# Layer-3 attention without transposes of the probabilities, and layer-1 projections in three fp16 products

## The reference

```python
# layer 1
q = (x @ Wq + bq).reshape(B, S, N_HEAD, HEAD_DIM)...   # k and v likewise
# layer 3
scores = jnp.einsum('bhqd,bhkd->bhqk', Q, K) / np.sqrt(D_HEAD)
scores = jnp.where(causal, scores, -jnp.inf)
attn = jax.nn.softmax(scores, axis=-1)
ctx = jnp.einsum('bhqk,bhkd->bhqd', attn, V)
```

## Time and profile before

| | |
|---|---|
| median of 3 runs | 2673.32 us (2670.43 to 2673.91) |
| the profiled execution's own time | 2670.77 us |
| its span | 2669.4 us |
| PE busy | 2510.5 us (94%) |
| PE weight loads busy | 2015.3 us (75%) |
| DVE busy | 2165.0 us (81%) |
| ACT busy | 2015.9 us (76%) |
| POOL busy | 1385.9 us (52%) |
| instructions | 57153 |

### The profile page before, as it was taken

How to read it: one execution, slowest core, us unless ns; L and a number is a source line. 1 busy time by engine, 2 the same in 40 slices (tenths; PEclk the granted TensorE clock), 3 DMA queues, 4 the chain that set the end, 5 groups by cost and what they waited for, 6 DMA issues and landing times.

```text
span 2669.4 us, 57153 instructions
## 1 busy us (share of the span) xinstructions
PE 2510.5 (94%) x19019; PEld 2015.3 (75%) x19019; DVE 2165.0 (81%) x7479; ACT 2015.9 (76%) x4435; POOL 1385.9 (52%) x1358
## 2 busy tenths in 40 slices
PE   7988999999999999999999999999999999999987
PEld 6756777777777777777777777777777777777766
DVE  6788888888888888888888888888888888878753
ACT  1456778887787787778788777878887887877864
POOL 2355565555556555555654555565455556545321
PEclk8889999999999999999999999999999999999999
DMA  5333233232333323233332322333232333322200
GB/s 201 104 103 94 84 101 93 85 93 78 89 90 100 94 85 93 78 90 90 101 93 84 94 78 89 90 101 93 84 94 78 90 90 105 98 82 73 56 17 21
DMA packets 178100, 237.29 MB, mean 89 GB/s; under 512 B 46032, under 2 KB 123856, under 8 KB 177424
## 3 DMA queue, kind: packets, MB, share of 16 engines
q1 hardware_dynamic: 177808, 233.64, 29.3%
HBM read 174.64 MB, written 8.45 MB: 69 GB/s over the span
## 4 chain that ended last, share of the span: by engine, by line
PE 63%; DVE 23%; ACT 6%; issue 4%; DMA 2%; SPq 2%; POOL 1%; DVEq 0%; POOLq 0%; ACTq 0%
PE bank L1397 17%; PE bank L1334 11%; PE bank L1420 8%; PE bank L1379 6%; PE bank L1436 6%; DVE PB L916 5%; PE bank L1410 4%; DVE PT L923 3%; PE bank L1322 2%; ACT AA L1181 2%; PE bank L1554 2%; PE bank L1386 2%; PE bank L1347 1%; ACT L1245 1%; DVE AA L1061 1%
## 5 line engine op out<-in xcount | busy, mean ns | idle before, releaser
L1155 ACT ACTIVATE PB<-PB,mx 128x256 f32<-128x256 f32 (+1 forms) x2048 | 835.6, 474 | 42.2 <-DVE mx L916 41.2
L556 POOL TENSOR_TENSOR BT<-BT,MN 128x1024 f32<-128x1024 f32 x256 | 545.1, 2139 | 259.2 <-DMA BT<-in_bias 254.8
L1420 PE MATMUL bank<-ident,PB 128*128 128x128 f32 x3584 | 490.4, 274 | 8.4 <-DVE PT L923 4.9
L1420 PEld LDWEIGHTS bank<-ident,PB 128*128 128x128 f32 x3584 | 423.1, 141 | 72.3 <-issue 11.7
L916 DVE CUSTOM_DVE_ANT_0 PB<-bank,caus,gain 128x128 f32<-128x128 f32 (+1 forms) x1024 | 371.0, 412 | 108.8 <-PE bank L1410 102.6
L1334 PE MATMUL bank<-TN,WS_w 128*128 128x256 f16 x3072 | 381.9, 275 | 21.8 <-ACT AA L1181 15.9
L916 DVE CUSTOM_DVE_ANT_0 PB<-bank,BT 128x256 f32<-128x256 f32 x1024 | 373.0, 419 | 29.7 <-PE bank L1410 28.1
L1410 PE MATMUL bank<-Ks,Qs 96*128 96x512 f16 (+1 forms) x1024 | 319.6, 358 | 37.3 <-DVE mx L916 26.0
L1334 PEld LDWEIGHTS bank<-TN,WS_w 128*128 128x128 f16 x3072 | 287.5, 98 | 85.2 <-ACT AA L1181 29.0
L923 DVE COPY PT<-bank 128x512 f32<-128x512 f32 (+1 forms) x512 | 315.6, 616 | 9.8 <-PE bank L1420 9.5
L1160 ACT ACTIVATE PT<-bank 128x512 f32<-128x512 f32 (+1 forms) x512 | 273.7, 535 | 28.1 <-PE bank L1420 27.6
(11 more groups left out here) (249 smaller groups left out, 4564.5 us busy)
## 6 DMA issues: line engine op xcount, KB each, us to landing
BT<-in_bias SPq DMA_DIRECT2D x256, 512.0 KB, 3.9
Qs<-QT SPq DMA_DIRECT2D x768, 32.0 KB, 1.9
Ks<-KT SPq DMA_DIRECT2D x1536, 16.0 KB, 1.8
XT<-in_xT SPq DMA_DIRECT2D x32, 256.0 KB, 2.8
X<-in_x SPq DMA_DIRECT2D x32, 256.0 KB, 3.0
AB<-ada_rows SPq DMA_DIRECT2D x32, 256.0 KB, 3.3
out<-Y SPq DMA_DIRECT2D x32, 256.0 KB, 2.0
BB<-in_wf SPq DMA_DIRECT2D x11, 256.0 KB, 3.8
```

The source lines that it names most:

```text
L556: G.op.tensor_tensor(v2(BT[k % 4]), v2(BT[k % 4]), MN[:, :].unsqueeze(1).broadcast_to([128, 2, 512]), ALU.add).then_inc(g_bt, 1)
L1155: S.op.activation(o, o, ACT.Exp, scale=-1.0, bias=mx[u.layer][:, c:c + 1]).then_inc(a_exp, 1)
L1420: last = T.op.transpose(bP[h][:, c * 128:c * 128 + 128], PB[(2 * u.D + q) % 6][:, h * 256 + k * 128:h * 256 + k * 128 + 128], ident[:, :])
```

## The change

Layer 3. The scores are still computed with queries in the partitions, but only for the row maxima: the DVE operations now write back into the score bank itself and their factor is -1. For each pair of units two small DVE operations (`mxs`) put the maxima as fp16 high and low parts into a small tile `Z`; two 128x128 fp16 products (`mt`) turn them into `bS[0]`; one ACT copy (`mq`) puts them as rows 96 to 103 under the queries in `Qs`. `Ks` has constants in those rows, written once (`key_rows`). `flip` of layer 3 is then a second score product with keys in the partitions, over 104 rows, with the maxima subtracted by the product itself: two fp16 matmuls a head (256 and 128 columns) in place of three fp32 transposes. One ACT exponential a head (`exp`, 384 wide, scale `gain3`) goes from PSUM straight to `PT`; `ev0` and `ev1` fall away in layer 3. GpSimd then sets the forbidden part of the two diagonal blocks to zero (`sel`), and `pv` waits for it. `Qs` and `Ks` have three buffers instead of two, and a buffer is free only after the second product.

Layer 1. q, k and v are three fp16 products each, as in layer 3. The weights are scaled and split at the start (`first_max`, `first_turn`, `first_spread`, `first_gains`, `first_rest`, on DVE, PE, GpSimd and ACT), after the rows of the second embedding exist, since their size sets the input's scale. The turned input gets a second part (`t1_lo`, DVE) and shares its buffer with layer 3's (`H1 = HB`), with waits for each other's value projections. The three weight loads are moved ahead of `rows` and the first `X`.

Ticks. `P`, `OWN` and `SPLIT` are new throughout; `PERIOD` stays 64. `WARM` is new: the products after each of the first sample's flips are gone, and some stand in samples 0 to 3 at other places (`keep`); the sum goes from 206 to 160 products.

```diff
@@ P and SPLIT (cut) @@
-    "score0": -2, "score1": -2, "bias0": -1, "bias1": -1, "exp0": 2, "exp1": 2, "flip0": 7, "flip1": 7, "ev0": 8,
+    "score0": 0, "score1": 0, "bias0": 0, "bias1": 1, "exp0": 4, "exp1": 5, "flip0": 8, "flip1": 8, "mxs": 2,
+    "mt": 3, "mq": 3, "sel": 11, "ev0": 10, "ev1": 9, "pv": 10, "cx": 15, "ct": 17, "pvn": 18, "ld_bt": -7,
...
-    "score1_3": -1, "bias1_3": 0, "exp0_3": 1, "exp1_3": 4, "ev1_3": 9, "ct_3": 17, "pvn_3": 17, "stack_3": -20,
+    "bias0_3": -1, "bias1_3": -1, "exp0_3": 11, "exp1_3": 12, "flip0_3": 9, "flip1_3": 10, "mxs_3": -1, "mt_3": 2,
+    "mq_3": 4, "sel_3": -9, "pv_3": 15, "cx_3": 16, "pvn_3": 19, "stack_3": -11,
@@ gpsimd @@
+                for u in unit_at(t, "sel"):
+                    if u.layer == 3:
+                        for h in range(2):
+                            p = flipped(u.D, h)[:, :].rearrange("p (k c) -> p k c", k=2)[:, :, 0:128]
+                            G.wait_ge(a_e3, head_of(nth(u), h))
+                            G.op.affine_select(out=p, in_=p, compare_op=ALU.is_ge, fill=0.0, base=0, pattern=[[0, 2], [1, 128]],
+                                               channel_multiplier=-1).then_inc(g_sel, 1)
@@ vector, attention @@
-                            V.op.tensor_tensor_reduce(PB[(2 * D + q) % 6][:, h * 256:h * 256 + w], bS[q][:, h * w:h * w + w],
-                                                      plus, -1.0 if x == 1 else gain3[:, :], 3.0e38, ALU.add, ALU.min,
+                                plus, dst = caus[:, 128:256] if q == 0 else caus[:, :], src
+                            V.op.tensor_tensor_reduce(dst, src, plus, -1.0, 3.0e38, ALU.add, ALU.min,
                                                       mx[x][:, c:c + 1]).then_inc(v_bias, 1)
+                for u in unit_at(t, "mxs"):
+                    if u.layer == 3 and u.n % 2 == 1:
...
+                        V.op.tensor_scalar(z[:, :, 96:100], m, 1.0 / 8192, None, ALU.mult).then_inc(v_mxs, 1)
+                        V.wait_ge(v_mxs, 2 * k + 1)
+                        V.op.scalar_tensor_tensor(out=z[:, :, 100:104], in0=m, scalar=1.0 / 8192, in1=z[:, :, 96:100],
+                                                  op0=ALU.mult, op1=ALU.subtract).then_inc(v_mxs, 1)
@@ vector, layer 1's input @@
+                for b in at(t, "t1_lo"):
+                    V.wait_ge(a_t1, b + 1)
+                    V.op.scalar_tensor_tensor(out=lo(H1), in0=bF[:, :], scalar=wp[:, 9:10], in1=hi(H1), op0=ALU.mult,
+                                              op1=ALU.subtract).then_inc(v_t1, 1)
@@ scalar @@
+                for u in unit_at(t, "mq"):
+                    if u.layer == 3 and u.n % 2 == 1:
+                        S.wait_ge(p_mt, nth(u) // 2 + 1)
+                        S.op.activation(Qs[stack_of(u.D)][96:104, :].rearrange("p (e n) -> p e n", e=2),
+                                        bS[0][96:104, 0:256].unsqueeze(1).broadcast_to([8, 2, 256]), ACT.Copy).then_inc(a_mq, 1)
...
+                            S.op.activation(flipped(u.D, q)[:, 0:384], bP[q][:, 0:384], ACT.Exp, scale=gain3[:, :]).then_inc(a_e3, 1)
...
-                    S.wait_ge(p_v[1], b)
-                    S.op.activation(H1[:, :], bF[:, :], ACT.Copy).then_inc(a_t1, 1)
+                    S.wait_ge(p_v[3], b - 2)
+                    S.wait_ge(v_p1, 15)
+                    S.op.activation(hi(H1), bF[:, :], ACT.Identity, scale=wp[:, 9:10]).then_inc(a_t1, 1)
@@ tensor, attention @@
                         T.wait_ge(v_bias, bias_of(D - 1, q, 1))
+                        if q == 0 and D > 0 and units[D - 1].layer == 3:
+                            T.wait_ge(a_mq, (nth(units[D - 1]) + 1) // 2)
...
+                        T.wait_ge(v_mxs, 2 * k + 2)
+                        T.wait_ge(g_const, 5)
+                        for q in range(2):
+                            last = T.op.matmul(half(bS[0], 0)[:, q * 128:q * 128 + 128], Z[k % 2][:, q * 128:q * 128 + 128],
+                                               identH[:, :], start=True, stop=True)
...
+                            T.wait_ge(a_mq, i // 2 + 1)
+                            T.wait_ge(v_kr, 13)
+                            for k in range(2):
+                                c = 512 * (u.n % 2) + 256 * h + 128 * k
+                                last = T.op.matmul(bP[h][:, 256 * k:256 + 128 * k], K[:, c:c + 128],
+                                                   Q[:, a + 128 * k:a + 256], start=True, stop=True)
...
+                        else:
+                            T.wait_ge(g_sel, head_of(nth(u), 1))
@@ tensor, projections @@
-                        return lin_N(ps, "v1", h) if name == "v" else lin_T(ps, f"{name}1", h)
+                    W, k0, a = (WP, 1536, 512 * "qkv".index(name)) if x == 1 else (WS[f"{name}3"], 512, 0)
+                    if name == "v":
+                        return split_N(ps, W, k0, a, h)
+                    return split_T(ps, W, k0, lambda m, k: a + k * 256 + m * 128, h)
...
-                        T.wait_ge(v_wq, 1)
-                        T.wait_ge(a_t1, b + 1)
+                        T.wait_ge(v_p1, 29)
+                        T.wait_ge(v_t1, b + 1)
```

More of the change, by code:

```diff
@@ L86 @@
     "score0", "score1", "bias0", "bias1", "exp0", "exp1", "flip0", "flip1", "ev0", "ev1",
-    "pv", "cx", "ct", "pvn", "ld_bt", "mask_add", "stack",
+    "pv", "cx", "ct", "pvn", "ld_bt", "mask_add", "stack", "mxs", "mt", "mq", "sel",
 }
@@ L366, in scale_of @@
             return ws[:, a:a + 1]
-        def blocks(layer):
-            return [(0, 0), (0, 1), (1, 1)] if layer == 3 else [(0, 0), (0, 1), (1, 0), (1, 1)]
         def width(layer, q):
@@ L1203, in scalar @@
                 attention(t)
+                for b in at(t, "split_p1_lo"):
+                    if b == 0:
+                        S.wait_ge(v_p1, 22)
+                        for i in range(3):
+                            S.op.activation(first_hi(i), raw1(i), ACT.Identity, scale=wp[:, 10 + i:11 + i]).then_inc(a_p1, 1)
                 for n in ORDER:
@@ L1286, in small, with warm, keep @@
                 return last
-            def warm(n, ps=bV):
-                for _ in range(n):
+            def warm(name, ps=bV):
+                for _ in range(WARM.get(name, 0)):
                     T.op.matmul(ps[:, 0:128], ident[:, :], ones[:, :], start=True, stop=True)
+            turns = []
+            def keep(piece, b):
+                if WARM.get(f"{piece}_{b}", 0):
+                    T.wait_ge(v_pvn, sum(turns))
+                    warm(f"{piece}_{b}")
             T.wait_ge(g_const, 4)
             T.wait_ge(v_set, 1)
-            warm(WARM["start"])
+            warm("start")
             T.wait_ge(d_wc0, 16)
@@ L1412, in attention @@
                                     start=True, stop=True).then_inc(p_score, 1)
+                for u in unit_at(t, "mt"):
+                    if u.layer == 3 and u.n % 2 == 1:
+                        k = nth(u) // 2
+                        T.wait_ge(v_mxs, 2 * k + 2)
[3 more added lines that the diff above has]
+                                               identH[:, :], start=True, stop=True)
+                        last.then_inc(p_mt, 1)
@@ L1413, in attention @@
                 for h in range(2):
                     for u in unit_at(t, f"flip{h}"):
-                        T.wait_ge(a_exp, bias_of(u.D, 1, h))
-                        T.wait_ge(v_ev if h else a_ev, u.D)
-                        if u.layer == 1 and u.b == 0:
-                            warm(WARM["flip"], bP[h])
-                        for c, (k, q) in enumerate(blocks(u.layer)):
-                            last = T.op.transpose(bP[h][:, c * 128:c * 128 + 128],
-                                                  PB[(2 * u.D + q) % 6][:, h * 256 + k * 128:h * 256 + k * 128 + 128], ident[:, :])
@@ L1499, in tensor @@
                         ada_rows()
-                        warm(WARM["adas"])
+                        warm("adas")
                 for b in at(t, "win"):
@@ L1579, in tensor @@
                         T.wait_ge(v_v[3], NB)
[L1580 removed]
+                        warm("o3", bF)
                 for b in at(t, "t4"):
```

331 lines of the change are left out of this document (241 added, 90 removed), and 139 rows, old and new, of tables (OWN, P).

## The result

The kernel after took 2694.46 us (median of 4 runs, 2687.29 to 2699.04) against 2672.10 us of the kernel before beside it (2670.43 to 2673.91). The ratio is 1.0081 with a 95% interval of 1.0057 to 1.0105: slower by 0.8%. The prediction said 2568 (2522 to 2632) and faster. The profiled execution took 2687.29 us, with a span of 2686.1 us, 16.7 more than before. It is the fastest of the four, so the trace holds 16.7 of the 22.4 us that lie between the medians.

What follows compares the result with a forecast made beforehand. PE's work was taken to set the turn (busy 2510.5 of 2669.4 us). From 2670.8 us, less 67 for layer 3 and 38 for layer 1, came 2565.8; with 2.5 for the runs' median, 2568 us, range 2522 to 2632.

Steps and rivals of the forecast that it cites:

- Sizes of PE's work: PE, layers 3 and 1: -67 and -38 us, together 105 us, 3.3 us a turn.
- PE's work sets the turn, and a microsecond of PE work removed is a microsecond of turn: Steady stage: PE, busy 74.75 of 77.85 us a turn, sets the time; removed PE work arrives in full.
- So the round trip fits if ACT takes it at once: Layer 3, `mxs`, `mt`, `mq` before the next unit's score: 1.16 us before queueing, hidden within a unit's 4.8 us.
- the rival's: Score after each layer-3 pair: round trip over `bS[0]` uncovered, 1.16 us or more, 148 us in all; chance 0.10.
- Sixteen selects a turn ... cost DVE under 2 us: POOL's layer-3 selects lengthen DVE sums with two SBUF inputs by under 2 us a turn; DVE has 12 to spare.
- `t1_lo` hidden: Layer 1's front: 0.7 us between copy and q, hidden by other PE work; uncovered it costs 22 us.
- The steady clock stays at 1.00: Steady stage: granted clock stays at 1.00 because PE stays busy over 95% of a turn.
- I take the two to cancel, with 8 us to either side: Head: 14 us of PE's warm products removed against some 10 us of splitting layer 1's weights, taken to cancel.
- Engine totals: Busy times after the change: PE near 2400 us, DVE near 2015, ACT near 1816, POOL near 1670.
- writing to the bank instead of SBUF is free: DVE, layer 3's maxima operations: 685 ns for bank<-bank, 690 for SBUF<-bank, so no added cost.
- no change: Rival: DVE's and ACT's order holds the turn and PE waits longer for the same total, 2670 us; chance 0.05.
- slower: Rival: round trip over `bS[0]` after each layer-3 pair not covered, 148 us, giving 2716 us; chance 0.10.

Runs made afterwards that it cites:

- two kernels without the chain: Before with one of three layer-3 transposes a head issued, 2639.26 us; after without `mxs`, `mt` and `mq`, 2641.57 us.
- the kernel without the chain: The kernel after without `mxs`, `mt`, `mq` and the waits for them, no maximum subtracted in layer 3's exponential: 2641.57 us, ratio 0.9884.
- The kernel with one flip: The kernel before with one transpose in place of three a head in layer 3: 2639.26 us, ratio 0.988.
- The kernel with the maxima in PSUM: The kernel after with layer 3's maxima in a free part of the score bank instead of SBUF: 2677.63 us, ratio 1.0022.

## Why the prediction was wrong

- **Sizes of PE's work: right.** 71.6 us a turn at full clock against 74.9 is the forecast's 3.3, and 56 and 113 ns are the distances of the new products of 128 and 256 columns. The Trainium skill ("TensorE: Matmul & The Clock Gate", section "Wait — 56ns, not 53.3ns?") gave 56 ns for 128 columns, and the trace agrees with 55 to 56.
- **"PE's work sets the turn, and a microsecond of PE work removed is a microsecond of turn": this step failed.** In two kernels without the chain 27% (31 of 113 us) and 26% (31 of 120 us) arrived, and 39 us came with no PE work removed at all. As an estimate by that share, the change's 105 us are worth 28; the second of the two has a slower head and slow stretches in it. Busy 94% was read as bound; the chain showed PE at 63%, and L1420 at 8% of the span, 214 us of the 490 that it is busy.
- **"So the round trip fits if ACT takes it at once": failed.** It costs 53 us, 0.41 us a pair. The mechanism is the rival's (place: between a pair's last maximum and the next unit's score), but that was priced at 148 us with an owed 105 of PE work behind it. The link that fails is DVE's end, not ACT's: PE waits at `mt`, up to 2.1 us, while in the whole run the scores waited 2.5 us for `mq` and the turned products 4.9. With a return of 28 us rather than 105, that wait decides from 28 / 128 = 0.22 us a pair, not from 0.82.
- **"Sixteen selects a turn ... cost DVE under 2 us": the wrong operations were looked at.** The two new small operations are themselves held by POOL, 356 and 534 ns against the 0.17 of the forecast, 114 us of DVE in place of 44; 15 to 17 us of the time go with it.
- **`t1_lo` hidden: not in the old order (50.5 us of waits), yes in the new.** Uncovered, PE waited 2.0 us for it, three times the 0.7 of the forecast.
- **"The steady clock stays at 1.00": failed.** Seven of sixteen turns have a stretch at the 1.2 GHz level and are 2.1 us longer than the others, 0.9 us a turn in the mean. The reason given, that PE stays busy, fell with the hidden waits: all 14 stretches between 320 and 2320 us stand right behind a wait for the maxima of 1.66 us or more, and in the kernel without the chain all 13 right behind its 2.2 us wait for ACT. The kernel with one flip, whose longest wait is 1.2 us, has none. The kernel with the maxima in PSUM has 19, all behind waits of 1.3 us, so the length of the wait alone doesn't decide. What else does stays open.
- **"I take the two to cancel, with 8 us to either side": failed by 17 us.** The first start came 4.2 us earlier, but the first sample's gap took 12.7 us longer, at a clock of 0.84 in place of 0.97, and the tail 8.2, at 0.89 in place of 0.98. The warm products that go were counted as PE work alone; whether the lower clock in the first gap comes of their absence isn't shown. The tail is back at 102.3 us without the chain.
- **Engine totals.** POOL 1569 against 1670: a select took 0.415 us, not 0.55. ACT 1909 against 1816: the exponential from PSUM took 581 ns, not 481, which is 45 of the 93 us; the rest has no single row. DVE 2130 against 2015: the small operations (+70), the operations that find the maxima (354 us against 383 before, 29 less where 80 were counted: with the constant factor the one of 256 columns still took 461 ns into the bank, against 417 for layer 1's into SBUF, so "writing to the bank instead of SBUF is free" doesn't hold for it, unless the mask makes the difference), and L1184, which takes 1900 ns where it took 769 before (+36). The busy times of single groups overlap in part and don't add up to an engine's total.

The sum again with what was measured, by turn: PE's work -3.3, its idle time +2.4, the turns with a slow stretch +0.9, together nothing; then head and tail, +17 us. The forecast gave the two rivals that come nearest, no change and slower, 0.15 together. The runs divide the 22.4 us between the medians in another way: without the chain the change is worth -31 us, and the chain costs +53. These two add up by construction and prove nothing more.

## What to carry to other kernels

An engine busy 94% in an in-order pipeline of three engines need not be the one that sets the time: compare its share of the chain that ended last (here 63%), and where the two differ, don't count removed work in full. Even the line's own share can be too much: the transposes had 214 of their 490 us on the chain, 44%, and 27% arrived. Before adding a round trip across engines, sum its links with what is queued ahead of each, and hold it against the part of the gain that arrives, not against all the work removed. Count with it what the clock may cost behind the wait. Issuing only a part of the instructions that the change is to remove gives that share before anything else is built.

## What the runs showed of the hardware

- A DVE operation on 128x8 elements with its input in SBUF takes 166 ns alone and up to 2055 beside POOL's 2.15 us operation; with its fp32 input in PSUM it took 166 in the mean of 128. The one with a single input is held as well (356 in the mean and up to 2151, 166 from PSUM). The Trainium skill ("SBUF — State Buffer", section "SBUF: two separate sides") says that a GpSimd operation that reads SBUF excludes a DVE one with two SBUF inputs, and any GpSimd operation one in a 2-port perf mode, for the whole instruction. The trace agrees for the two-input form; whether the one-input form ran in such a mode no run shows.
- The readout that follows each DVE operation with a maximum took 82 ns in before; in after it took 82 behind the operations that write to SBUF and 0.14 us behind those that write back to PSUM (timeline above), 110 ns in the mean.
- The exponential of 384 elements from PSUM, with a per-partition scale, took 581 ns where a copy of that shape took 481.
- PE fell to the 1.2 GHz level for 3.4 us at a time in the midst of the steady stage, in seven of sixteen turns of after and in none of before. In all of the kernels here with such stretches in the steady stage (101 stretches in eight kernels), each stands close behind or at the end of an idle time of PE of 1.16 us or more; before, with none over 0.7 us, has none. Half of the long idle times of after are not followed by one.
